# Counting the edges of a graph with one-hot matmuls: three buffers per group of one-hots, and both register reads ahead of the two key fetches

## The reference

```python
def gcn_layer(h, W, b):
    h = h @ W
    msg = norm[:, None] * h[row]
    agg = jax.ops.segment_sum(msg, col, num_segments=N)
    return agg + b
...
w_m = (efeat @ W_msg + b_msg).reshape(E, in_f, -1)
w_a = (efeat @ W_attn + b_attn).reshape(E, in_f, -1)
h_src = feat[src][:, :, None]
e1, e2 = w_m * h_src, w_a * h_src
attn = ex / denom[dst]          # a softmax of e2 over the edges of one destination
ft = jax.ops.segment_sum(e1 * attn, dst, num_segments=N)
```

## Time and profile before

| what | value |
|---|---|
| median of 3 runs | 2864.72 us (2863.4 to 2865.85) |
| the profiled execution: time / span | 2865.78 us / 2864.0 us |
| DVE, PE, ACT, POOL busy, share of the span | 77%, 72%, 49%, 44% |
| counting, first one-hot to last copy | 42 to 667 us |

### The profile page before, as it was taken

How to read it: one execution, slowest core, us unless ns; L and a number is a source line. 1 busy time by engine, 2 the same in 40 slices (tenths; PEclk the granted TensorE clock), 3 DMA queues, 4 the chain that set the end, 5 groups by cost and what they waited for, 6 DMA issues and landing times.

```text
span 2864.0 us, 38979 instructions
## 1 busy us (share of the span) xinstructions
PE 2068.3 (72%) x5640; PEld 752.6 (26%) x5641; DVE 2210.6 (77%) x4456; ACT 1415.6 (49%) x4968; POOL 1269.6 (44%) x1556
## 2 busy tenths in 40 slices
PE   3757777777797377777777777778776777777672
PEld 1111111113234133333333333333332333333230
DVE  5867888885101398898888888889888888989883
ACT  4123333311010466666666666666666666666652
POOL 2100000032555665655555555555555555555543
PEclk9555555557897588888888888888887888888886
DMA  2000000000000110000000000000000000000010
GB/s 33 10 25 0 0 0 0 0 1 10 17 11 13 15 10 9 10 9 9 9 8 9 9 9 9 9 9 9 9 9 9 9 9 9 9 9 9 9 7 9
DMA packets 87256, 26.29 MB, mean 9 GB/s; under 512 B 63117, under 2 KB 84223, under 8 KB 87103
## 3 DMA queue, kind: packets, MB, share of 16 engines
q0 software_dynamic: 37824, 18.62, 5.5%
q1 hardware_dynamic: 49327, 6.96, 1.6%
q10 hardware_dynamic: 80, 0.43, 0.1%
HBM read 23.30 MB, written 2.51 MB: 9 GB/s over the span
## 4 chain that ended last, share of the span: by engine, by line
PE 32%; issue 23%; DVE 21%; DVEq 15%; POOLq 4%; POOL 4%; DMA 1%; ACT 1%; ACTq 0%; PEldq 0%; SPq 0%; PEld 0%
PE psum_acc L794 25%; DVE eo L1387 6%; DVEq L1434 6%; PE bank L656 5%; DVE eo L1425 4%; DVE hot L1127 3%; DVE hot L1125 2%; PE pw L784 2%; DVE rden L1441 2%; DVEq L1148 1%; POOLq L564 1%; DVEq L1474 1%; DVEq L1404 1%; DVE top L1402 1%; POOL shared L519 1%
## 5 line engine op out<-in xcount | busy, mean ns | idle before, releaser
L794 PE MATMUL psum_acc<-eo,ident 128*128 128x512 f32 x1856 | 1086.0, 740 | 375.2 <-DVE eo L1425 375.2
L615 POOL DMA_INDIRECT nbr<-table,rec x960 | 916.8, 955 | 488.5 <-issue 257.9
L981 ACT ACTIVATE eo<-pw,nbr 128x32 f32<-128x32 f32 x3776 | 683.8, 405 | 0.0
L794 PEld LDWEIGHTS psum_acc<-eo,ident 128*128 128x128 f32 x1856 | 432.9, 240 | 926.1 <-issue 909.0
L656 PE MATMUL bank<-hot 128*128 128x500 bf16 x974 | 464.1, 610 | 174.0 <-DVE hot L1127 143.1
L1387 DVE TENSOR_TENSOR eo<-pw,nbr 128x1024 f32 (+1 forms) x357 | 425.2, 1220 | 95.4 <-PE pw L784 92.3
L1125 DVE TENSOR_SCALAR hot<-iota_key,near_key 128x500 bf16<-128x500 f16 x974 | 341.0, 350 | 120.6 <-PE bank L656 62.6
L970 ACT ACTIVATE eo<-eo 128x2048 f32<-128x2048 f32 x117 | 223.5, 1910 | 210.0 <-DVE eo L1416 210.0
L784 PE MATMUL pw<-wk,termsT 100*128 100x512 bf16 x954 | 289.4, 385 | 43.5 <-issue 43.1
L1425 DVE TENSOR_TENSOR eo<-eo x232 | 274.1, 1223 | 48.0 <-issue 45.5
L862 ACT CAST counts<-bank 128x500 f32 x158 | 90.7, 575 | 424.0 <-PEq L674 422.1
(11 more groups left out here) (219 smaller groups left out, 1619.7 us busy)
## 6 DMA issues: line engine op xcount, KB each, us to landing
nbr<-table,rec POOLq DMA_INDIRECT x960, 2.4
rec<-unit_recs SPq DMA_DIRECT2D x122, 8.0 KB, 1.8
attr<-in_edge_attr_dram,rec POOLq DMA_INDIRECT x120, 2.8
unit_recs<-place SPq DMA_DIRECT2D x27, 64.0 KB, 1.6
shared<-key_row SPq DMA_DIRECT2D x1, 1600.0 KB, 6.5
counts<-in_dst_dram SPq DMA_DIRECT2D x1, 448.0 KB
counts<-in_src_dram SPq DMA_DIRECT2D x1, 448.0 KB
place<-in_src_dram,at_i POOLq DMA_INDIRECT x26, 2.6
```

The source lines that it names most:

```text
L615: pool.indirect_dma_start(nbr[:, b, j * FEAT:(j + 1) * FEAT], None, table, bass.IndirectOffsetOnAxis(ap=rec[:, b, j:j + 1], axis=0)).then_ ...
L794: mm = pe.matmul(psum_acc[:], ident[:], eo[:, ring, j * 2 * CH:(j + 1) * 2 * CH], start=(j == 0), stop=(j == SLOT - 1), skip_group_check=True)
L981: done = act.activation(eo[:, ring, lo:lo + wide], pw[:, j - 4, c * wide:(c + 1) * wide], ACT.Copy, scale=nbr[:, held, j * FEAT + c:j * FE ...
```

## The change

`hot` gets seven slots in place of five (`BASE + 1`): each of the three groups of a window has its own two, and the tail tile has the seventh. DVE and PE name the slot by `a` and not by `at % 2`, and the initial value of `s_hot_free` is 3 in place of 2. The count read moves from behind group 2 into `near`, right behind the start read and in front of the two key copies; its value stays in one of two registers (`tiles[v]`) until the branch of that window. Room for the slots comes from `edge_key` and `edge_low` (822 columns in place of 896), from `win_row_g`, which now lies in `hot`, and from `identh`, which is gone: `add_loops` takes the bfloat16 identity. `win_count` gets a 159th entry.

```diff
-        edge_key = sb("edge_key", [P, EG * P], F32, conv)
-        edge_low = sb("edge_low", [P, EG * P], BF16, conv)
+        edge_key = sb("edge_key", [P, NB + DEPTH], F32, conv)
+        edge_low = sb("edge_low", [P, NB + DEPTH], BF16, conv)
...
-        win_row_g = sb("win_row_g", [1, 2, NWIN], F32, conv)
...
-        identh = sb("identh", [P, P], F16, conv)
...
-        hot = sb("hot", [P, (2 * GROUP + 1) * (NG * WIN + P)], BF16, conv)
+        hot = sb("hot", [P, (BASE + 1) * (NG * WIN + P)], BF16, conv)
...
+        win_row_g = hot_f[0:1, 0:2 * NWIN].rearrange("p (k n) -> p k n", n=NWIN)
...
-                                mm = count(at % 2 * GROUP + k, a == 0 and k == 0)
+                                mm = count(a * GROUP + k, a == 0 and k == 0)
...
-                                count(2 * GROUP, False).then_inc(s_tail_free, 1)
+                                count(BASE, False).then_inc(s_tail_free, 1)
...
-                act.copy(to[:], flat[:, 0:EG * P]).then_inc(s_keys, 1)
+                act.copy(to[:], flat[:, 0:NB + DEPTH]).then_inc(s_keys, 1)
...
-            dve.sem_inc(s_hot_free, 2)
+            dve.sem_inc(s_hot_free, BASE // GROUP)
...
-            dve.tensor_copy(identh[:], ident[:])
...
+            tiles = [dve.alloc_register(f"dve_count{v}") for v in range(2)]
...
                 t0 = dve.value_load(win_start[0:1, bass.ds(window, 1)], min_val=0, max_val=NB)
+                dve.reg_mov(tiles[v], dve.value_load(win_count[0:1, bass.ds(window, 1)], min_val=1, max_val=DEPTH))
                 dve.tensor_scalar(near_key[v][:], edge_key[:, bass.ds(t0, DEPTH)], win_off[:, bass.ds(window, 1)],
                                   None, ALU.add)
...
-                                hot_row = one_hot(at % 2 * GROUP + k, v, slice(a * GROUP + k, a * GROUP + k + 1))
+                                hot_row = one_hot(a * GROUP + k, v, slice(a * GROUP + k, a * GROUP + k + 1))
...
-                        n = dve.value_load(win_count[0:1, bass.ds(i * 2 + v, 1)], min_val=1, max_val=DEPTH)
+                        n = dve.snap(tiles[v], min_val=1, max_val=DEPTH)
...
-                                one_hot(2 * GROUP, v, bass.ds(k, 1)).then_inc(s_tail, 1)
+                                one_hot(BASE, v, bass.ds(k, 1)).then_inc(s_tail, 1)
...
-                    dve.tensor_tensor(here, here, identh[:].unsqueeze(1).broadcast_to([P, n, P]), ALU.add)
+                    dve.tensor_tensor(here, here, identb[:].unsqueeze(1).broadcast_to([P, n, P]), ALU.add)
```

More of the change, by code:

```diff
@@ L138, in gnn_kernel @@
         win_row_f = sb("win_row_f", [1, 2, NWIN], F32, conv)
-        win_row_g = sb("win_row_g", [1, 2, NWIN], F32, conv)
         win_start = sb("win_start", [1, NWIN + 1], I32, conv)
-        win_count = sb("win_count", [1, NWIN], I32, conv)
+        win_count = sb("win_count", [1, NWIN + 1], I32, conv)
         planes = sb("planes", [1, 1], I32, conv)
@@ L150, in gnn_kernel @@
         y3 = gp2_flat.bitcast(F32)[:, 0:NG * FEAT].rearrange("p (t f) -> p t f", t=NG)
-        hot = sb("hot", [P, (2 * GROUP + 1) * (NG * WIN + P)], BF16, conv)
-        hot_key = hot[:, 0:(2 * GROUP + 1) * NG * WIN].rearrange("p (k n) -> p k n", n=NG * WIN)
-        hot_low = hot[:, (2 * GROUP + 1) * NG * WIN:].rearrange("p (k n) -> p k n", n=P)
+        hot = sb("hot", [P, (BASE + 1) * (NG * WIN + P)], BF16, conv)
+        hot_key = hot[:, 0:(BASE + 1) * NG * WIN].rearrange("p (k n) -> p k n", n=NG * WIN)
+        hot_low = hot[:, (BASE + 1) * NG * WIN:].rearrange("p (k n) -> p k n", n=P)
         near_key = [sb(f"near_key{v}", [P, DEPTH], F32, conv) for v in range(2)]
@@ L1023, in _ @@
             dve.memset(win_start[:, NWIN:NWIN + 1], 0)
+            dve.memset(win_count[:, NWIN:NWIN + 1], 1)
             dve.memset(win_off[:, NWIN:NWIN + 1], 0.0)
@@ L1112, in plane_tables @@
                 dve.tensor_copy(win_start[:, 0:NWIN], win_row_g[:, 0, :])
-                dve.tensor_copy(win_count[:], win_row_g[:, 1, :])
+                dve.tensor_copy(win_count[:, 0:NWIN], win_row_g[:, 1, :])
                 dve.drain().then_inc(s_planes, 1)
```

## The result

| kernel | median | runs |
|---|---|---|
| before | 2865.59 us (2863.4 to 2868.29) | 8 |
| changed | 2875.26 us (2872.66 to 2877.16) | 8 |

The ratio is 1.0028 (1.0018 to 1.0038): the change costs 9.7 us, or 0.28%, where 1.9 us of gain were forecast. The profiled execution took 2872.82 us, 7.0 more than the one of before and 2.4 less than the median of the changed kernel.

A forecast was written before the change was run, and what follows sets the result against it. DVE was taken to set the pace in counting. Windows gave -1.4 us, the long wait -1.6, the first fetch +0.7, the last group 2 +0.4: together -1.9, median 2862.8 us; range reads of 0.62 (2850) to 0.78 (2875), plus 1 us.

The forecast's parts named there:

- Part 1: Window's end without the count read: group 2 to next window 0.85 for 1.11 us (even), 0.99 for 1.57 (odd).
- if odd windows still take 3.9: Sign that the prediction is wrong: odd windows staying at 3.9 us, where 3.74 was forecast.
- Part 2: Count read in the key fetch, uncovered: 0.69 plus 0.01 us, moving the key copy to 2.55 (even) and 2.52 (odd).
- Rival (a): Count read costs more inside the fetch than behind group 2; slower by over 0.2% from 0.75 us on; chance 0.22.
- Rival (b): Count read costs less in the fetch: 2850 us at 0.62, 2800 at its lower bound of 0.30; chance 0.18.
- Part 3: Third buffer: no plain window waits for PE; group 2 starts 0.23 behind the key copy, at 2.78 (even), 2.75 (odd).
- rival (d): The change fails on the path: a wait for PE stays at group 2 or a window's start; chance 0.03.
- Tails: Windows with a tail one-hot: even 4.13 us, odd 4.66, the odd tail's 1.06 to the next window staying.
- The long wait: DVE's 21.56 us wait for the bank ACT keeps: group 2 and tail done inside it, saving 1.6 us once.
- The start of counting: First key fetch, ahead of counting and uncovered: costs 0.7 us more.
- `add_loops`: Adding bfloat16 to float16 costs 0 more; were the rate halved, 1.8 us more.
- Rival (c): Both reads lie hidden under one-hots and only the gains are left: 2752 us; chance 0.02.

The follow-up runs named there:

- experiment 4: Changed kernel with the register copy for the window-end branch taken behind group 1, ahead of the wait; 2869.54 us, ratio 1.0012 to the kernel before.
- Experiment 3: Changed kernel with one more count read in the key fetch, its value unused; 2969.63 us, ratio 1.036 to the kernel before.
- experiment 2: Changed kernel with the count read back behind group 2, so only the three buffers are left; 2832.72 us, ratio 0.9892 to the kernel before.
- experiment 5: Changed kernel with start read behind group 0, count read behind group 1, the s_hot wait behind both; 2773.94 us, ratio 0.9682 to the kernel before.
- experiment 9: Changed kernel with only the s_hot wait moved behind both reads, which stay behind group 1; ratio 0.9744 to the kernel before.
- experiment 10: Changed kernel with the s_hot wait behind both reads and the branch's register copy taken ahead of the reads; ratio 0.9735 to the kernel before.
- experiment 7: Changed kernel with four register moves added ahead of counting, meant to shift later instructions; 2875.6 us, ratio 1.0032 to the kernel before; nothing was shifted.
- experiment 8: Changed kernel with eight register moves added ahead of counting, meant to shift later instructions; 2873.85 us, ratio 1.0026 to the kernel before; nothing was shifted.
- experiment 11: Changed kernel with one register move added ahead of counting; 2974.59 us, single run, in a round where the kernel before took 2968.57; nothing was shifted.
- experiment 12: Changed kernel with two register moves added ahead of counting; 2979.54 us, single run, in a round where the kernel before took 2968.57; nothing was shifted.
- Experiment 6: Changed kernel with both reads placed under the one-hots, ahead of the s_hot wait, but two alternating buffers; 2867.1 us, ratio 1.0004 to the kernel before.
- experiment 1: Changed kernel with two alternating buffers as before, so only the moved count read is left; 2895.81 us, ratio 1.0102 to the kernel before.

## Why the prediction was wrong

**Part 1, the end of a window: right for even windows, wrong for odd ones, and that is the step that failed.** Even: 0.85 forecast, 0.85 measured. Odd: 0.99 forecast, 1.146 measured. The forecast let the branch run 0.13 behind group 2's first one-hot and the next window 0.86 behind the branch. What runs at 0.126 is the MOVE of `snap`, which the diff shows and the listing of the instructions' order does not: the branch does not follow the last one-hot directly, as was said there. The MOVE is worth 0.07 (experiment 4). Then the pause of 0.12, a term that the sum did not have, stands ahead of the branch. From the branch on it takes 0.83, not 0.86. With the 0.02 by which group 2 comes later, an odd window is 3.916 and not 3.74: 66 plain odd windows by 0.176 are 11.6 us. The prediction named this sign of its own failure, "if odd windows still take 3.9", and they do.

**Part 2, the count read in the fetch: right.** 0.69 + 0.01 forecast; the key copy moved by 0.69 in even windows and 0.71 in odd ones. Experiment 3 gives the read without its register step as 0.62, the other part of the same figure. Rival (a), whose sign came true, is not the cause: it needed 0.75. It had 0.22 and got the direction right by luck. Rival (b) falls as well.

**Part 3, the third buffer: right.** Group 2 at 2.78 and 2.77 (2.78 and 2.75 forecast), with no wait for PE in a plain window; rival (d) falls.

**Tails: priced too high.** Odd tails take 4.42 in place of 4.66: of the 1.06 between the tail's one-hot and the next window, which was to stay, 0.80 is left. 12 x 0.24 = 2.9 us less. The 0.54 that the earlier trace rows put down to PE was no wait for it: PE had freed that slot at least 0.75 us before, and in experiment 2, with three buffers and the read at its old place, the 1.06 stays. It is the steps of the tail and of the loop's end, which start earlier once the count read no longer stands ahead of them. Even tails: 14 x 0.07 = 1.0 less.

**The small terms.** The long wait gave 1.3 in place of 1.6. The start of counting costs 1.35 in place of 0.7: the second read is 0.6 of it, and the start read itself runs 0.7 later (41.57 against 40.84), which I had set at 0. The change does not show as the cause of that: in the other kernels with the moved read it runs at 40.6 to 41.5. `add_loops` took 1759 ns against 1758: mixed 16-bit types lose nothing, so the rule of the Trainium skill, "VectorE: DVE Perf Modes", section "What auto-detection actually checks", holds here.

**The sum again.** -1.9 forecast, +11.6 (odd ends), -2.9 -1.0 (tails), +0.3 (long wait), +0.65 (start) make +6.75. The means of the plain windows lie 0.01 above their medians, 1.6 us for 131 windows, and that makes the 8.3 seen at the last copy. Later stages give 1.3 back, to 7.0. This is the difference of the two profiled executions; the medians differ by 2.7 more, which no trace here takes apart. The granted clock was 0.55, not the "still 0.50"; DVE sets the pace, so it changed little.

**Where the expected gain went.** The forecast of hardly any change was a small difference of two large terms, and the experiments show both: 31 us from the third buffer alone, 39 us paid for the read behind a wait that leaves it uncovered. Rival (c), both reads hidden at 2752 us, had 0.02, and rightly for this change: for it the wait must stand behind the reads. In experiment 5 it does, and the time is 2773.94. What I took from the earlier trace rows, that the start read alone fills group 1's 0.85, holds only while the reads wait for group 0; DVE's queue had room for more.

**Where the pause of 0.12 stands.** It is at the odd branch in the changed kernel and in experiment 4, at the odd key copy in experiment 3, ahead of the odd MOVE in 5 and 9, at the odd branch in 10, and in no even window. Counted from the start of DVE's program, this is one place. Experiment 3 has three steps more in each key fetch (12,882 records against 12,405, 477 = 3 x 159), hence nine more ahead of the end of an odd window: in the fetch ahead of the loop, in the even window and in the odd one. And its pause is at the key copy, nine instructions ahead of the branch. Experiments 4 and 10 put nothing more ahead of the branch, and the pause is at the branch. Experiments 5 and 9 have one step more in each fetch of the loop (12,563), so two more; the place falls on the last one-hot instruction, directly ahead of the MOVE, which runs 0.267 behind group 2 and not 0.126. In the kernel before and in experiment 2 the branch stands five instructions earlier, and the place falls among the tail's first instructions, which plain windows jump over. Their odd windows with a tail show it there: 0.26 us pass between the address steps of the tail's two one-hot instructions, 0.13 in even windows. That is the same place to within two instructions.

This was read from the traces after the runs, and it is the theory of experiments 7, 8, 11 and 12, which these did not test. Experiment 6 neither shows the pause nor speaks against it: its group 2 waits for PE, and the sequencer with it.

**Left open:** what happens at that place, and whether a real shift of the whole stream would move the pause.

## What to carry to other kernels

A register read costs its 0.6 to 0.7 us only where the engine's queue runs empty beside it, so ask of each read which wait stands ahead of it in program order, and put the wait behind the reads, directly ahead of the first instruction whose data need it: here that one line was worth more than both edits of the change. Count among these waits those of the engine instructions ahead of the read, even where the engine itself is never idle for them. Where a forecast is the small difference of a large gain and a large cost, measure each half alone; the third buffer was worth 21, 31 or 93 us by what stood beside it. Compare a window's steps one by one with the code, a copy of a register included. Look in the trace whether an edit reached the program: four kernels here were meant to differ and did not. And before a row's "wait for PE" is believed, look when PE had freed what is waited for.

## What the runs showed of the hardware

**A one-hot that waits for a semaphore also holds DVE's sequencer ahead of the steps behind it.** In experiment 1 the start read ran 0.13 behind the waiting one-hot's start (451.93 against 451.80), while behind one-hots that wait for nothing it ran with five of eight still to start in even windows and seven in odd ones (experiment 9). It is held even where DVE is not idle: in 44 windows of experiment 9 the read's first step follows PE's release of group 1's slot by 0.05 to 0.06 us, with three more one-hot instructions between the waiting one and the read. My note on the queue in the prediction (rival c) had only the second half.

**The granted clock does not tell a matmul's duration by itself.** Of experiment 3, the busy time by stretch, at 1.00, the level of 2.4 GHz:

```profile
220.00:560.00 340.00, 213.24 (x447) 42.33 (x445) 213.98 (x1032) 105.39 (x139) 2.94 (x12) 1.00 0.02 5
```

Its counting matmuls there take 622 ns in the median, as they do in the changed kernel at 0.55 and in the one before at 0.50. In experiment 5, where a window takes 3.1 us, the median is 383 ns at 0.80, with PE busy for less of the time (222 of 340 us against 248 in the changed kernel). What decides between 622 and 383 was not tried by itself.
